# A windowed-attention and mixture kernel: the last transformed keys made at the head of the fourth slot, the convolution's taps spread over three slots

## What is computed

```
t = layernorm(x)
q, k, v = t @ w_q, t @ w_k, t @ w_v            # 8 heads of 32
attn  = softmax(q k^T * scale) v               # in windows of 8x8 points
local = conv3x3(v, w_local) + b_local          # nine taps
x  = x + (attn + local) @ w_out + b_out
t2 = layernorm(x)
gate, top-2 of 8 experts; x = x + sum_of_two w_e * (gelu(t2 @ W1[e] + b1[e]) @ W2[e] + b2[e])
```

## Time and profile before

| | us |
|---|---|
| median of 3 runs | 467.13 (467.08 to 471.24) |
| the profiled execution | 466.88 |
| its span in the trace | 465.1 |
| first part, to the first expert block | about 328 |
| PE busy in the span | 411.9 (89%) |
| DVE busy | 358.3 (77%) |
| ACT busy | 333.6 (72%) |
| POOL busy | 302.1 (65%) |

### The profile page before, as it was taken

How to read it: one execution, slowest core, us unless ns; L and a number is a source line. 1 busy time by engine, 2 the same in 40 slices (tenths; PEclk the granted TensorE clock), 3 DMA queues, 4 the chain that set the end, 5 groups by cost and what they waited for, 6 DMA issues and landing times.

```text
span 465.1 us, 12477 instructions
## 1 busy us (share of the span) xinstructions
PE 411.9 (89%) x3921; PEld 279.7 (60%) x3921; DVE 358.3 (77%) x1256; ACT 333.6 (72%) x889; POOL 302.1 (65%) x386
## 2 busy tenths in 40 slices
PE   8899879789877978978978969878899999999995
PEld 8354335344444535535535435434899999999995
DVE  4579878876697797797797779889885788788632
ACT  2566667777687786766777756441998899998894
POOL 4243342755744787787787765755777777777775
PEclk9999899999999999989999979989999999999999
DMA  9917500000000000000000000102432222222220
GB/s 225 213 47 176 122 1 1 1 1 1 2 1 1 7 20 19 12 25 13 13 25 20 7 29 26 36 24 70 103 90 74 71 58 57 59 74 72 74 55 0
DMA packets 36169, 22.42 MB, mean 48 GB/s; under 512 B 13649, under 2 KB 33856, under 8 KB 36105
## 3 DMA queue, kind: packets, MB, share of 16 engines
q1 hardware_dynamic: 30264, 14.70, 14.1%
q0 software_dynamic: 4960, 6.45, 4.2%
q10 hardware_dynamic: 880, 0.48, 0.6%
HBM read 13.07 MB, written 9.27 MB: 48 GB/s over the span
## 4 chain that ended last, share of the span: by engine, by line
PE 62%; DVE 18%; issue 9%; ACT 5%; POOL 5%; DMA 0%; POOLq 0%; ACTq 0%; DVEq 0%
PE bank L1644 16%; PE bank L1460 9%; PE bank L1630 8%; PE bank L1489 6%; PE bank L1478 5%; DVE mx L1153 4%; PE bank L1502 4%; DVE sm L1161 2%; DVE sc L1156 2%; ACT aa L753 2%; PE bank L1516 2%; PE bank L1398 1%; DVE st L1185 1%; POOL out L656 1%; PE bank L1463 1%
## 5 line engine op out<-in xcount | busy, mean ns | idle before, releaser
L641 POOL TENSOR_TENSOR pn<-pe_,rs 128x512 f32<-128x512 f32 x64 | 67.6, 1057 | 87.1 <-DVE rs L1164 86.9
L1460 PE MATMUL bank<-aa,bd 64*64 64x256 f32 x512 | 72.2, 400 | 33.0 <-ACT aa L753 31.6
L617 POOL DMA_INDIRECT rows_hbm<-rowb,posu x64 | 65.2, 1019 | 22.6 <-issue 18.5
L656 POOL DMA_INDIRECT out<-bt,zs x63 | 63.0, 1001 | 20.1 <-issue 14.6
L1153 DVE TENSOR_REDUCE mx<-bank 128x8 f32<-128x512 f32 x64 | 43.8, 685 | 41.2 <-PE bank L1460 41.0
L1460 PEld LDWEIGHTS bank<-aa,bd 64*64 64x64 f32 x512 | 32.9, 135 | 66.7 <-ACT aa L753 37.0
L1463 PE MATMUL bank<-pt,bt 64*64 64x256 f32 x512 | 72.2, 401 | 0.7 <-ACT pt L767 0.7
L762 ACT COPY zs<-bank 128x512 f32<-128x512 f32 x64 | 37.4, 584 | 35.0 <-PE bank L1463 34.3
L793 ACT ACTIVATE pe_<-sc 128x512 f32<-128x512 f32 x64 | 40.6, 635 | 22.9 <-DVE sc L1156 22.6
L1156 DVE TENSOR_TENSOR sc<-bank,mx 128x512 f32<-128x512 f32 x64 | 44.3, 691 | 2.2
L1276 DVE SCALAR_TENSOR_TENSOR bt<-bank,zs 128x64 f32<-128x64 f32 x91 | 25.5, 280 | 24.8 <-PE bank L1644 23.2
(11 more groups left out here) (293 smaller groups left out, 1051.7 us busy)
## 6 DMA issues: line engine op xcount, KB each, us to landing
zs<-rows_hbm SPq DMA_DIRECT2D x91, 66.0 KB, 1.9
wloc<-in_L_conv_w_local SPq DMA_DIRECT2D x2, 1152.0 KB, 9.1
rows_hbm<-zrow SPq DMA_DIRECT2D x1, 1914.0 KB, 13.2
x_sb<-in_x SPq DMA_DIRECT2D x3, 512.0 KB, 10.8
wloc<-in_L_ffn_W SPq DMA_DIRECT2D x2, 512.0 KB, 6.5
rows_hbm<-rowb,posu POOLq DMA_INDIRECT x64
out<-bt,zs POOLq DMA_INDIRECT x63, 2.3
wrec<-in_w2b SPq DMA_DIRECT2D x1, 520.0 KB, 5.4
```

The lines of the kernel that those rows point to most:

```text
L617: nc.gpsimd.indirect_dma_start(out=rows_hbm, out_offset=bass.IndirectOffsetOnAxis(ap=posu[:, t:t + 1], axis=0), in_=rowb[:, t], in_offset= ...
L641: nc.gpsimd.tensor_tensor(pn[:, v % 2, :].rearrange("p (h j) -> p h j", h=HEADS), pe_[:, v % 2], rs[:, v % 2].unsqueeze(2).broadcast_to([P ...
L656: nc.gpsimd.indirect_dma_start(out=out, out_offset=bass.IndirectOffsetOnAxis(ap=idx_j, axis=0), in_=ob[:, j % LANES], in_offset=None, boun ...
L1460: scored = nc.tensor.matmul(dots[v % 2][same, w * 2 * P:(w + 1) * 2 * P], xq[same, t % 2, 2 * v + w], aa[same, t % 2, :, j0:j0 + WT], star ...
```

## The change

Computed is the same. Eight things move:

- PE: keys 2 and 3 of the next group stand at the head of slot 3, ahead of that slot's scores, instead of behind its transposition.
- PE: the nine taps stand three in slot 1 (before L1539), three at the end of slot 2, three at the end of slot 3.
- ACT, slot 2: keys 0 and 1 are both copied ahead of the exponential (before: one ahead, one behind).
- ACT, slot 3: keys 2 and 3 are both copied at the head of the slot, ahead of `zs`, `pt` and the exponential (before: 2 between `pt` and the exponential, 3 behind it).
- ACT, slot 1: `xsp` is copied ahead of `pt`.
- ACT: `xs` and `gate_out` of the early batches come ahead of `pt`.
- ACT: `xw` is copied at the end of slot 1 instead of the end of slot 0.
- `ranks_out` of the early batches stays behind `pt` and ahead of the exponential.

```diff
--- before.py
+++ after.py
@@ -752,39 +752,47 @@
                 dst = aa[:, nxt % 2, pr, :].rearrange("p (n ty c) -> p ty n c", n=2, c=WSZ)
                 nc.scalar.mul(dst, turn[a_turn[pr]][:].rearrange("p (ty n c) -> p ty n c", n=2, c=WSZ), 1.0 / WS).then_inc(a_ready, 1)
 
+            def values_out(g, u):
+
+                t, v = tile(g, u - 4)
+                if real(t):
+                    wait(act, z_done, at(t, TG, v + 1))
+                    wait(act, att_done, at(t, 1, -1))
+                    nc.scalar.copy(zs[:, t % 2, v], zb[:].rearrange("p (a b) -> p a b", a=PAIRS)).then_inc(z_ready, 1)
+
             def body(g):
                 nxt = sh(g, 1)
                 for u in range(TG):
-                    t, v = tile(g, u - 4)
-                    if real(t):
-                        wait(act, z_done, at(t, TG, v + 1))
-                        wait(act, att_done, at(t, 1, -1))
-                        nc.scalar.copy(zs[:, t % 2, v], zb[:].rearrange("p (a b) -> p a b", a=PAIRS)).then_inc(z_ready, 1)
-                    t, v = tile(g, u - 3)
-                    if real(t):
-                        wait(act, pt_done, at(t, TG, v + 1))
-                        wait(act, z_done, at(t, TG, v - 1))
-                        nc.scalar.copy(pt[:, v % 2], ptb[:].rearrange("p (a b) -> p a b", a=PAIRS)).then_inc(pt_ready, 1)
+                    if u == 3 and real(nxt):
+                        keys_out(nxt, 2)
+                        keys_out(nxt, 3)
+                    values_out(g, u)
                     for b, k in due("xs", g, u):
                         if b <= 4:
                             second_xs(b)
                     for b, k in due("gate_out", g, u):
                         if b <= 4:
                             gate_out(b)
-                    if real(nxt):
-                        if u == 1:
-
-                            wait(act, x16_done, at(nxt, 1, 1))
-                            wait(act, conv_done, at(nxt, 1, -2))
-                            if is_step(nxt, 0):
-                                act.wait_ge(zeroed, 1)
-                            src = half(turn[X16])
-                            nc.scalar.copy(xsp[:, nxt % 3, :, 1:1 + HI, 2:2 + WI],
-                                           src.rearrange("p (m y c) -> p m y c", m=IG, y=HI)).then_inc(xsp_ready, 1)
-                            for b_, k in due("ranks_out", g, u):
-                                ranks_out(b_)
-                    if u in (2, 3) and real(nxt):
-                        keys_out(nxt, 2 * (u - 2))
+                    if u == 1 and real(nxt):
+
+                        wait(act, x16_done, at(nxt, 1, 1))
+                        wait(act, conv_done, at(nxt, 1, -2))
+                        if is_step(nxt, 0):
+                            act.wait_ge(zeroed, 1)
+                        src = half(turn[X16])
+                        nc.scalar.copy(xsp[:, nxt % 3, :, 1:1 + HI, 2:2 + WI],
+                                       src.rearrange("p (m y c) -> p m y c", m=IG, y=HI)).then_inc(xsp_ready, 1)
+                    t, v = tile(g, u - 3)
+                    if real(t):
+                        wait(act, pt_done, at(t, TG, v + 1))
+                        wait(act, z_done, at(t, TG, v - 1))
+                        nc.scalar.copy(pt[:, v % 2], ptb[:].rearrange("p (a b) -> p a b", a=PAIRS)).then_inc(pt_ready, 1)
+                    if u == 1 and real(nxt):
+                        for b, k in due("ranks_out", g, u):
+                            ranks_out(b)
+                    if u == 2 and real(nxt):
+                        keys_out(nxt, 0)
+                        keys_out(nxt, 1)
                     t, v = tile(g, u)
                     if real(t):
                         wait(act, sub_ready, at(t, TG, v + 1))
@@ -792,8 +800,6 @@
                         wait(act, sum_ready, at(t, TG, v - 1))
                         nc.scalar.activation(pe_[:, v % 2], sc[:, v % 2], ACT.Exp,
                                              scale=SCALE / XS / XS).then_inc(exp_ready, 1)
-                    if u in (2, 3) and real(nxt):
-                        keys_out(nxt, 2 * (u - 2) + 1)
                     if is_step(g, 0):
                         conv_weights_out(u)
                     if is_step(g, -1) and u == 3:
@@ -816,7 +822,7 @@
                         wait(act, att_done, at(prv, 1, 1))
                         wait(act, yt_done, at(prv, 1, -1))
                         nc.scalar.activation(ys[:, prv % 2, :], attb[:], ACT.Identity, scale=1.0 / (XS * WS), bias=ybias[:, 0:1]).then_inc(y_ready, 1)
-                    if u == 0 and real(g):
+                    if u == 1 and real(g):
 
                         wait(act, z_done, at(g, TG, -TG))
                         wait(act, xswap_done, at(g, 1, 1))
@@ -1505,6 +1511,11 @@
             def body(g):
                 nxt, prv, prv2 = sh(g, 1), sh(g, -1), sh(g, -2)
                 for u in range(TG):
+                    if u == 3 and real(nxt):
+                        wait(pe, a_ready, at(nxt, PAIRS, 1))
+                        do_a(nxt, 2)
+                        wait(pe, a_ready, at(nxt, PAIRS, 2))
+                        do_a(nxt, 3)
                     scores_and_values(g, u)
                     transposed(g, u)
                     nb = nxt % 2
@@ -1529,7 +1540,7 @@
                                                            hl[:, nb, k].rearrange("p a c -> p (a c)"), ident16[:])
                             last.then_inc(x16_done, 1)
                         if real(prv):
-                            taps(prv, 0, 4)
+                            taps(prv, 0, 3)
                         if real(nxt):
 
                             wait(pe, xsp_ready, at(nxt, 1, 1))
@@ -1538,8 +1549,6 @@
                             window_read(g)
                             nc.tensor.matmul(turn[XT][:], both16[:].rearrange("p k c -> p (k c)"), xsp[:, nxt % 3, :, 1:1 + HI, 2:2 + WI],
                                              start=True, stop=True).then_inc(xt_done, 1)
-                        if real(prv):
-                            taps(prv, 4, TAPS)
                         for b, k in due("ranks", g, u):
                             if b < 4:
                                 wait(pe, xsp_ready, at(nxt, 1, 1))
@@ -1569,12 +1578,8 @@
                                 pe.wait_ge(sub_ready, NT)
                                 pe.wait_ge(w1_ready, TG)
                                 hold(8)
-                    if u == 3:
-                        if real(nxt):
-                            wait(pe, a_ready, at(nxt, PAIRS, 1))
-                            do_a(nxt, 2)
-                            wait(pe, a_ready, at(nxt, PAIRS, 2))
-                            do_a(nxt, 3)
+                    if u in (2, 3) and real(prv):
+                        taps(prv, 3 * u - 3, 3 * u)
                     if is_step(g, -1) and u == 3:
 
                         pe.wait_ge(rows_in, 16 * 3)
```

## The result

The changed kernel takes 451.27 us (median of 4 runs, 449.9 to 452.81) against 467.11 (4 runs, 466.62 to 471.24): a ratio of 0.9617, interval 0.9568 to 0.9666 (the two medians by themselves give 0.966, inside it). In some executions of any of these kernels the granted clock is lower and the time longer; the ratios leave those out, the medians and ranges keep them. The forecast was 448, its own range 442 to 453. The profiled execution took 449.90 with a span of 448.1 and is compared with the 466.88 and 465.1 of before: 17.0 us less.

What follows compares the result with a forecast made beforehand. Hand-offs were taken to bound the first part (PE waiting 31.6 us for copied keys, DVE 41.0 for scores), PE the second. Gains by group summed to 21.2, less a tenth 19: 466.9 - 19 = 448 us, own range 442 to 453.

Steps and rivals of the forecast that it cites:

- group 1: The stretch from 36.6 to 54.5 us, DVE busy 16.84 of 17.90: a gain of 0.5 us.
- groups 4, 5: Groups with little DVE work (10.86, 10.62) that become PE's: gains of 1.75 and 1.4 us.
- group 14: DVE is continuous through slots 2 and 3, but the ranks and scores that follow start earlier: 2.4 us gained.
- the tenth: A tenth taken off the summed 21.2 us, since the layout allows only the known waits, leaving 19.
- Slot 1 and 2, six taps gone: Six taps leave slot 1, so `mx` of slot 2 starts at 4.8 instead of 5.6: 0.8 us gained.
- Keys ahead of the exponential: Keys all copied by 8.7, slot 3's `mx` at 8.9, next group's scores at 10.1 instead of 12.3; the 2.35 us wait gone.
- The exponentials' delay costed at nothing: Exponentials lose 0.5 us in slot 2, up to 1 in slot 3, at no cost: DVE wants the sum 3 us later.
- the three store pairs: Pairs where POOL stores rows, floor near 30.4 us: 2.7 gained per pair, 8.1 together, and 0.9 of clock.
- POOL or ACT paces: Rival, chance 0.27: store pairs keep 33.5 us, about 455; slow ACT hand-offs, 458; more POOL and DVE meetings, 456.
- Clock: Granted clock 0.50 from 200.70 to 204.10, behind a wait for keys: about 0.9 us counted back once.
- Slower: Rival, chance 0.06: slot 3's scores stand behind two keys and three taps, `pt` holds slot 2's: about 8 us, 475.
- the wait only moves: Rival, chance 0.09: slot 2's scores gain only half of 1.2, DVE waits at slot 3 instead: 467, within 4.

Runs made afterwards that it cites:

- Moving one copy back: The changed kernel with only ACT's copy of keys 3 put back behind slot 3's exponential: 462.61 us, ratio 0.988.
- The change once more: The changed kernel rerun unchanged as the yardstick for its variants on another chip: 451.34 us, ratio 0.9625.
- the kernel before with POOL's two edits: The kernel before, with L963 and L964 one slot later and each POOL store behind its slot's division: 469.48 us against 469.39, ratio 0.9982.
- the stores moved on: The changed kernel with `fall` later and stores behind the divisions, its stores now in slots 20 to 25 instead of 18 to 25: 452.38 us, ratio 0.964.

## Why the prediction was right, and where its terms were off

The forecast's mechanism held: 451.27 lies in its own range, 3.3 above 448. Term by term, from the stretches of both kernels:

| stretch | forecast gain | measured |
|---|---|---|
| group 1 | 0.5 | 2.9 |
| groups 2, 3 | 1.5, 1.5 | 0.7, 1.8 |
| groups 4, 5 | 1.75, 1.4 | 0.2, 1.7 |
| pair 6/7 | 3.1 | 3.3 |
| pairs 8/9, 10/11, 12/13 | 2.7, 3.6, 2.7 | 1.1, 2.7, 1.1 |
| group 14 | 2.4 | 1.7 |
| head, drain | 0 | -0.2 |

The measured column makes 17.0, the forecast's 21.2, less a tenth, 19. That the number came this near was in part luck: the other terms together were 6.6 too high. Group 1, in which the profiled execution of before had a fall of the clock, gave back 2.4 of that, and the tenth, taken off for no wait in particular, another 2.1.

- **Slot 1 and 2, six taps gone.** Right: `mx` of slot 2 starts 4.8 us behind the slot-1 scores (118.98 - 114.19), as laid out.
- **Keys ahead of the exponential.** Right: slot 3's `mx` at 9.0 (8.9), the next scores at 10.5 (10.1), 0.4 later than laid out since they wait for `sc`. Moving one copy back cost 11.3 us. PE's waits for keys were to fall under 8 us and fell to 1.6. Those left stand at the head of slot 3 of odd groups, where keys 2 wait for the copy of keys 0: 0.4 us to 136.59, which is 22.4 behind 114.19. The layout had 0.5, to 22.4.
- **The exponentials' delay costed at nothing.** Right: DVE's `sm` waits for no exponential anywhere in the list of waits. The delay itself was smaller than laid out: in group 6 the exponentials of slots 2 and 3 start 0.3 and under 0.1 us behind the end of their `sc`, not 0.5 to 1. In the store pairs they do come late, by POOL and not by the copies.
- **The failed size: the three store pairs.** I took 2.7 each and 0.9 of clock, 9.0 in all; 4.9 came. I had a floor for POOL, some 30.4 us of work and gaps, and this didn't bind: POOL is busy 25.87 to 27.35 of 32.4. What bound was *where* POOL's work lies. Two instructions of DVE are held 1.6 us a pair longer than before (`fall` behind three POOL instructions in a row); issuing them later gave 1.0 a pair. And ACT's exponentials stand behind POOL's stores and divisions, which makes `pt` late and PE's next scores wait 1.6 us; the stores behind the divisions gave 1.0 more in the first pair and nothing in the others, where the wait for `nm` took the old one's place. With both edits the pairs are 30.4 to 31.3, near the 30.8 that the term meant. The rival "POOL or ACT paces" had the place and the mechanism of the two engines' exclusion right, but foresaw many more meetings of 0.7 us; what came was one long one a pair, 1.6 us net. This is the term that a look at POOL's next three instructions, not at its busy sum, would have sized.
- **Group 1, 2.4 too little, much of it not the change's.** PE's 114 matmuls took 15.07 us at clock 0.90 before and 13.53 at 1.00 now; the profiled execution of the change has its fall in the head instead (0.50 from 8.8 to 15.6). Other kernels tell how much is the order's. The change once more has 16.10 us in this stretch, and the kernel before with POOL's two edits, which first act behind 130 us, has 17.40, both at 1.00. Between these two the gain is 1.3, not 2.9. The rest goes, as far as these runs tell, with which execution was profiled.
- **Group 4, 1.55 too much.** DVE was to have little to do there, but comes in late from group 3's work (busy 13.51 of 14.60); 12.77 of the 15.40 us are DVE's, not the 10.86 of the earlier trace rows. The work had only moved from one stretch to the next: over groups 1 to 4 DVE was busy 56.3 us with 147 instructions before, and is 56.0 with 146 now.
- **Clock.** In pair 10/11 it rose from 0.95 to 1.00, and PE's busy time fell by 1.2 (0.9 counted). In group 14 it is 0.91, not 0.84. But in group 2 it is 0.91 as before. The rule of the Trainium skill's page "TensorE: Matmul & The Clock Gate", Part 1, that the clock follows how busy the array has been, agrees with the first two. That all falls would go was so in part only. In group 2 PE's wait of 3.2 us for keys is gone, but one of 2.16 for `xw` has come, and the fall follows it. This is the condition that the prediction set and did not follow up: moving `xw` costs nothing "while slot 1's exponential isn't late". In group 14 PE waits 2.93 us for `pt` before the fall; with `xw` in slot 0 it waits 2.82, no fall comes and the group takes 17.1 us and not 18.7. So such a wait does not bring a fall each time.
- **"Slower" and "the wait only moves".** Neither came. `mx` waits 22 times, not 30, and for half as long. `pt` does hold the scores five times, 8.3 us in all, which my layout had at nothing. All but 0.5 of it lies in the store pairs and in group 14, the very terms that came out too large.

Left open: how the store pairs get to 30.4 and below all three. With both edits the even groups 10 and 12 are held by the statistic `nm` behind one store more, as the rows of that run show; with the stores moved on, that wait goes and the odd groups pay more. No run places the stores so that both are spared. Nor was any run made for group 14, 0.7 short.

## What to carry to other kernels

On an engine that runs its queue in order, put a copy that depends on nothing late ahead of the instruction that waits for the late engine: one copy's place was 11 of 16 us here. Look at what the moved copy itself lands behind, in every group: `xw` landed behind a table load in one of them. When such a wait goes, what meets behind it next is not the busiest engine's total but two engines' instructions that now fall side by side. So lay out the changed stretch with the neighbour engine's next few instructions in it, and undo each part by itself before crediting it.

## What the runs showed of the hardware

A VectorE subtraction of 128x8 with two inputs in SBUF took 2.34 us and not 0.16 in each of three pairs: it ended with the last of three GpSimd instructions in a row (0.62, 0.61 and 1.03 us), not with the first. With `fall` later and the stores behind the divisions, a comparison of the same size took 1.50 us beside two in a row, in two pairs. The earlier trace rows had 0.91 beside a single division. That these two engines exclude each other is what the Trainium skill's page "SBUF — State Buffer", section "Who interferes with whom", says. The traces agree, and in them the VectorE instruction is held by several in succession.

The head of the kernel differs by up to 3 us between executions of the same work: group 2's `attended` starts at 49.8 us in the change and at 52.7 in the kernel with `fall` later, whose edit first acts behind 127 us. PE's pace is part of it: the same eight score matmuls near 17 us last 1.08 us in the one and 1.97 in the other. With medians of few runs that hides edits of 1 us, and the pair's length is the better measure.
